# Channels ordered by depth, bands built in two stages, and four PSUM banks in a fused convolution and attention kernel

## The reference

```python
x = _L0_conv_ref(x, L0_conv_W, L0_conv_b)                 # adds a position term
x = x + _L1_conv_ref(_gn(x), ...)
t = _to_tokens(x)
t = t + _L2_attn_ref(_ln_t(t), ...)                       # below
t = t + _L2_ffn_ref(...); t = t + _L3_attn_ref(...); t = t + _L3_ffn_ref(...)

# _L1_conv_ref: 8 heads of 8 channels over 256 tokens
q = xt @ Wq.T + bq;  k, v = halves of xt @ Wkv.T + bkv
q, k = (relu(q) + 1e-06) / scale, (relu(k) + 1e-06) / scale
q, k = each cubed, and scaled back to its own norm
kv_state = einsum('bjc,bjd->bcd', k, v)                   # per head
out = einsum('bic,bcd->bid', q, kv_state) / (q . sum(k) + 1e-06)
out = out + depthwise 5x5 convolution of v + dwc_b        # 8 filters, shared by the heads
return out @ Wproj.T + bproj

# _L2_attn_ref: tanh(H W' + b) gives a score e for each token; then, over the batch,
# C[t] = sum_{s<=t} softmax_{s<=t}(e[s]) * H[s]
```

## Time and profile before

| | us |
|---|---|
| median of 3 runs | 1475.98 (1475.4 to 1478.64) |
| span of the profiled execution | 1099.1 |
| median less span | 376.9 |
| stage one | 0 to 33.4 |
| stage two | 33.4 to 110.8 |
| stage three | 110.8 to 158.9 |
| stage four | 158.9 to 230.4 |
| later stages | 230.4 to 1099.1 |

### The profile page before, as it was taken

One profiled execution on the slowest core, in us unless ns is written; L12 is line 12 of the kernel. 1 busy time (PEld: TensorE's weight loads), 2 busy tenths in 40 slices (PEclk: granted clock), 3 DMA queues, 4 the chain that ended last, 5 costly groups with the idle time before them and its releaser, 6 DMA issues. The chain is left out here.

```text
span 1099.1 us, 12315 instructions
## 1 busy us (share of the span) xinstructions
PE 602.3 (55%) x3397; PEld 478.4 (44%) x3397; DVE 698.3 (64%) x1125; ACT 410.9 (37%) x688; POOL 589.1 (54%) x558
## 2 busy tenths in 40 slices
PE   2789776213310588477279841598155884783000
PEld 2774773213310587477144431244044774772000
DVE  6482474686670598478877589775458893885111
ACT  1454225131300576467224232143135773771000
POOL 0242141420777778777477600677205777775775
PEclk9979887555555799699679865698557996996555
DMA  3000991000211698688261100011104985882211
GB/s 106 7 1 1 207 354 25 0 1 0 94 46 52 198 292 243 198 249 241 57 103 24 24 1 0 38 46 53 53 22 147 299 259 185 261 250 62 55 35 38
DMA packets 126199, 118.91 MB, mean 108 GB/s; under 512 B 24917, under 2 KB 111525, under 8 KB 126147
## 3 DMA queue, kind: packets, MB, share of 16 engines
q1 hardware_dynamic: 56104, 54.93, 16.5%
q10 hardware_dynamic: 53659, 38.16, 11.9%
q0 software_dynamic: 16384, 25.20, 8.4%
HBM read 42.73 MB, written 44.04 MB: 79 GB/s over the span
## 5 line engine op out<-in xcount | busy, mean ns | idle before, releaser
L980 POOL DMA_INDIRECT blocks_x<-L_ffnmhl,L_ffnslot x192 | 198.5, 1034 | 162.9 <-DVE L_ffnslot L1233 105.0
L992 POOL DMA_INDIRECT gy_last<-blocks_y,L_ffnslot x128 | 129.7, 1013 | 57.0 <-issue 38.4
L992 POOL DMA_INDIRECT L_ffngy<-blocks_y,L_ffnslot x128 | 128.1, 1001 | 39.0 <-issue 39.0
L1033 PE MATMUL L_ffnps<-ident,L_ffnxb 128*128 128x128 f32 x384 | 65.5, 300 | 128.3 <-DMA L_ffnxb<-blocks_x 118.6
L1249 DVE TENSOR_TENSOR L_ffnwr<-L_ffnwb,L_ffnwr 128x640 fp32r<-128x640 f32 x96 | 79.2, 826 | 69.7 <-ACT L_ffnwr L1102 68.9
L1049 PE MATMUL L_ffnps<-L_ffnxt,L_ffnwr 128*128 128x256 f32 x768 | 118.3, 299 | 3.0 <-ACT L_ffngate L1118 2.4
L980 POOL DMA_INDIRECT blocks_x<-L_ffnlhl,L_ffnslot x64 | 66.3, 1036 | 82.3 <-DVE L_ffnslot L1233 63.1
L1102 ACT CAST L_ffnwr<-L_ffnwb 128x640 fp32r<-128x640 f32 x96 | 69.8, 727 | 108.5 <-issue 86.5
L1033 PEld LDWEIGHTS L_ffnps<-ident,L_ffnxb 128*128 128x128 f32 x384 | 44.7, 151 | 138.7 <-issue 107.8
L1049 PEld LDWEIGHTS L_ffnps<-L_ffnxt,L_ffnwr 128*128 128x128 f32 x768 | 101.4, 197 | 4.5 <-issue 3.2
L1060 PE MATMUL L_ffnps<-L_ffnwr,L_ffnhlo 128*128 128x128 f32 x384 | 92.8, 280 | 0.0
(11 more groups left out here) (289 smaller groups left out, 1387.4 us busy)
## 6 DMA issues: line engine op xcount, KB each, us to landing
L_ffnwb<-WR SPq DMA_DIRECT2D x192, 160.0 KB, 3.4
L_ffnxb<-blocks_x ACTq DMA_DIRECT2D x96, 256.0 KB
blocks_x<-zeros SPq DMA_DIRECT2D x2, 6144.0 KB, 29.9
blocks_y<-L_ffnyb ACTq DMA_DIRECT2D x96, 128.0 KB
WR<-in_L_ffn_w SPq DMA_DIRECT2D x10, 512.0 KB, 11.0
blocks_x<-L_ffnmhl,L_ffnslot POOLq DMA_INDIRECT x192, 2.2
Xc<-in_x SPq DMA_DIRECT2D x4, 512.0 KB, 7.5
L_ffngy<-blocks_y,L_ffnslot POOLq DMA_INDIRECT x128
```

The costliest lines, as they stand in the source:

```text
L980: pool.indirect_dma_start(self.XD[part], bass.IndirectOffsetOnAxis(self.slot[:, part, k, t:t + 1], 0), self.HL[part][:, t].rearrange("p a ...
L992: pool.indirect_dma_start(self.GY[part][:, k, t], None, self.YD[part], bass.IndirectOffsetOnAxis(self.slot[:, part, k, t:t + 1], 0)).then_ ...
L1033: ins = pe.transpose(ps[:, j % 2, s * P:(s + 1) * P], self.xb[:, j % 4, s], K["ident"][:])
```

## The change

1. Channels inside a head group are ordered by depth and then head: the weights, the bias rows, `epsv`, Wproj and the mask are permuted as they are built. One depth of V is then runs of eight adjacent floats. For Wproj, GpSimd permutes a copy (`w3` to `w2`), and TensorE's transposes wait for it.
2. Bands 0 to 3 are built in stage one: `rowk` is copied earlier, TensorE makes the bands behind the matmul for the means, into banks 4 to 7, and ScalarE copies them ahead of its normalisations. `sely` is loaded in stage one, ahead of four tables on SP's queue. Bands 4 to 7 are built inside the loop over half tiles, ahead of half tiles 16, 20, 24 and 28.
3. The convolution uses the four banks 4 to 7, so TensorE may be four ahead of ScalarE. ScalarE's list is written anew.
4. `mask` and `bp` are loaded in stage two, and SP waits for them there; VectorE's wait in stage three is gone.
5. `add` goes over X in X's order, and BH is the strided operand.

```diff
+BANDS = 4
+
...
+def by_depth(ap):
+    return ap.rearrange("p (h d) -> p d h", d=HD)
+
+
+def heads(ap):
+    return ap.rearrange("p (d h) -> p d h", d=HD)
...
-                pool.memset(K["ones"][:].bitcast(F32), 1.0)
+                then(pool.memset(K["ones"][:].bitcast(F32), 1.0))
+                pool.wait_ge(big_w, 16 * 12)
+                pool.tensor_copy(w2[C:P].rearrange("p a (d h) -> p a d h", d=HD),
+                                 w3[C:P].rearrange("p a (h d) -> p a d h", d=HD)).then_inc(turned, 1)
+                pool.wait_ge(turned, 1)
...
-                    act.dma_start(w2[C:P, half, :], A["L1_conv_Wproj"]).then_inc(big_w, 16)
+                    act.dma_start(w3[C:P, half, :], A["L1_conv_Wproj"]).then_inc(big_w, 16)
...
+                def bands(k):
+                    pj, i4 = k // 4, (k % 4) * 4
+                    act.wait_ge(band_ps, k + 1)
+                    act.copy(T[:, pj, :, i4 * 8:(i4 + 4) * 8].rearrange("p a (u b) -> p u a b", b=8),
+                             ps[:, 4 + k, :].rearrange("p (u a b) -> p u a b", u=4, b=8))
+
+                for k in range(BANDS):
+                    bands(k)
                 act.wait_ge(norm_ready, 1)
                 for q in range(1, Q, 2):
                     act.activation(xn[:, q, :], Xc[:, q, :], ACT.Identity, bias=nmr[:, q:q + 1], scale=rs[:, q:q + 1])
...
                 pe.wait_ge(big_w, 16 * 12)
+                pe.wait_ge(turned, 1)
                 pe.transpose(ps[:, 1, 0:P], w1[:].rearrange("p a c -> p (a c)"), K["ident"][:])
                 pe.transpose(ps[:, 1, P:2 * P], w2[:].rearrange("p a c -> p (a c)"), K["ident"][:]).then_inc(wt_ready, 1)
...
                           start=True, stop=True).then_inc(gm_ready, 1)
+                pe.wait_ge(sely_in, 16)
+                pe.wait_ge(rowk_sb, 1)
+                for k in range(BANDS):
+                    pj, i4 = k // 4, (k % 4) * 4
+                    for u in range(4):
+                        s0 = (HH - 1 - (i4 + u)) * 8
+                        ins = pe.matmul(ps[:, 4 + k, u * P:(u + 1) * P], sely[:, pj, s0:s0 + P],
+                                        rowk[:].rearrange("k d a b -> k (d a b)"), start=True, stop=True)
+                    ins.then_inc(band_ps, 1)

             @block.vector
...
-                dve.tensor_scalar(epsv[:], sp_[:, 7, :], 1e-6, None, ALU.mult)
+                dve.tensor_scalar(heads(epsv[:]), by_depth(sp_[:, 7, :]), 1e-6, None, ALU.mult)
...
+                dve.wait_ge(rowk_ps, 1)
+                dve.tensor_copy(rowk[:], ps[0:KS * WW, 2, 0:P].rearrange("k (b a d) -> k d a b", a=2, d=8)
+                                ).then_inc(rowk_sb, 1)
...
                     rows = slice(b2 * C, b2 * C + C)
                     for k in range(2):
-                        dve.tensor_tensor(wqkv[rows, k, b2, :], ps[rows, 1, k * C:(k + 1) * C], sp_[rows, 7, :], ALU.mult)
-                    dve.tensor_copy(wqkv[rows, 2, b2, :], ps[rows, 1, 2 * C:3 * C])
+                        dve.tensor_tensor(heads(wqkv[rows, k, b2, :]), by_depth(ps[rows, 1, k * C:(k + 1) * C]),
+                                          by_depth(sp_[rows, 7, :]), ALU.mult)
+                    dve.tensor_copy(heads(wqkv[rows, 2, b2, :]), by_depth(ps[rows, 1, 2 * C:3 * C]))
                     dve.tensor_copy(wproj[rows, b2, :], ps[rows, 1, 3 * C:4 * C])
...
-                    then(dve.tensor_copy(brow[row], braw[row]))
-                then(dve.tensor_tensor(brow[row], braw[row], brow[row].bitcast(F32), ALU.subtract))
-                dve.wait_ge(rowk_ps, 1)
-                dve.tensor_copy(rowk[:], ps[0:KS * WW, 2, 0:P].rearrange("k (b a d) -> k d a b", a=2, d=8))
+                    then(dve.tensor_copy(sorted_heads(brow[row]), unsorted_heads(braw[row])))
+                then(dve.tensor_tensor(sorted_heads(brow[row]), unsorted_heads(braw[row]),
+                                       sorted_heads(brow[row]).bitcast(F32), ALU.subtract))
...
+        def of_depth(t, par, d):
+            return t[:, :, par, 0:2 * C].rearrange("p q (b c) -> p q b c", c=C)[:, :, :, d * NH:(d + 1) * NH]
...
-                sp.dma_start(sely[:], A["k_sely"]).then_inc(loaded, 16)
                 sp.dma_start(dwb[:], A["L1_conv_dwc_b"].rearrange("(a d) -> a d", a=1).to_broadcast([P, HD])
                              ).then_inc(loaded, 16)
+                sp.dma_start(mask[:], A["k_mask"]).then_inc(mask_in, 16)
+                for b2 in range(2):
+                    sp.dma_start(bp[:, b2, :], A["L1_conv_bproj"].rearrange("(a c) -> a c", a=1).to_broadcast([P, C])
+                                 ).then_inc(mask_in, 16)
+                sp.wait_ge(mask_in, 48)
...
+                def bands(k):
+                    pj, i4 = k // 4, (k % 4) * 4
+                    if k >= BANDS + 2:
+                        pe.wait_ge(band_sb, k - BANDS - 1)
+                    for u in range(4):
+                        s0 = (HH - 1 - (i4 + u)) * 8
+                        ins = pe.matmul(ps[:, 6 + k % 2, u * P:(u + 1) * P], sely[:, pj, s0:s0 + P],
+                                        rowk[:].rearrange("k d a b -> k (d a b)"), start=True, stop=True)
+                    ins.then_inc(band_ps, 1)
+
                 for i in range(NT2):
+                    if i >= 16 and i % 4 == 0:
+                        bands(BANDS + i // 4 - 4)
...
-                for k in range(8):
-                    pj, i4 = k // 4, (k % 4) * 4
-                    if k >= 2:
-                        pe.wait_ge(band_sb, k - 1)
...
-                    ins.then_inc(band_ps, 1)
                 pe.wait_ge(v_ev, Q // 2)
-                pe.wait_ge(band_sb, 8)
+                pe.wait_ge(band_sb, 8 - BANDS)

                 for k in range(2 * HD):
                     d, pi = k // 2, k % 2
-                    if k >= 2:
-                        pe.wait_ge(conv_ev, k - 1)
+                    if k >= 4:
+                        pe.wait_ge(conv_ev, k - 3)
                     for pj in range(2):
-                        ins = pe.matmul(ps[:, 4 + k % 2, 0:B * NH], T[:, pj, 2 * d + pi, :],
-                                        V[:, :, pj, d:2 * C:HD], start=(pj == 0), stop=(pj == 1))
+                        ins = pe.matmul(ps[:, 4 + k % 4, 0:B * NH], T[:, pj, 2 * d + pi, :],
+                                        of_depth(V, pj, d), start=(pj == 0), stop=(pj == 1))
                     ins.then_inc(conv_mm, 1)

...
                     act.copy(T[:, pj, :, i4 * 8:(i4 + 4) * 8].rearrange("p a (u b) -> p u a b", b=8),
                              ps[:, 6 + k % 2, :].rearrange("p (u a b) -> p u a b", u=4, b=8)).then_inc(band_sb, 1)

                 def conv(k):
                     d, pi = k // 2, k % 2
                     act.wait_ge(conv_mm, k + 1)
-                    act.activation(FM[:, :, pi, d:2 * C:HD], ps[:, 4 + k % 2, 0:B * NH].rearrange("p (q h) -> p q h", q=Q),
+                    act.activation(of_depth(FM, pi, d),
+                                   ps[:, 4 + k % 4, 0:B * NH].rearrange("p (q b h) -> p q b h", q=Q, b=2),
                                    ACT.Identity, bias=dwb[:, d:d + 1]).then_inc(conv_ev, 1)

                 for g in range(G):
...
-
-                        act.wait_ge(loaded, 32)
-                        bands(0)
-                        bands(1)
+                    if g >= 2:
+                        bands(BANDS + 2 * g - 4)
+                        bands(BANDS + 2 * g - 3)
                     act.wait_ge(qk_ev, (g + 1) * QG)
                     square(g)
                     if g == G - 1:
-                        bands(2)
+                        act.wait_ge(loaded, 16)
+                        conv(0)
+                        conv(1)
                     if g >= 1:
                         sixths(g - 1)
                     if g == G - 1:
-                        bands(3)
+                        for k in range(2, 5):
+                            conv(k)
                     if g >= 2:
                         root(g - 2)
-                for k in range(4, 8):
-                    bands(k)
+                for k in range(5, 8):
+                    conv(k)
                 sixths(G - 1)
-                conv(0)
+                conv(8)
                 root(G - 2)
-                for k in range(1, 4):
+                for k in range(9, 12):
                     conv(k)
                 root(G - 1)
-                for k in range(4, 2 * HD):
+                for k in range(12, 2 * HD):
                     conv(k)

             def cube(eng, g):
...
-                dve.wait_ge(loaded, 48)
                 for q in range(Q):
                     dve.wait_ge(kv_mm, q + 1)
-                    dve.tensor_tensor(BD[:, q, 0:P], ps[:, 4 + q % 2, 0:P], mask[:], ALU.mult)
-                    dve.tensor_tensor(BD[:, q, P:W], mask[:, 0:P:HD], ps[:, 4 + q % 2, P:P + 1].to_broadcast([P, 2 * NH]),
+                    m = mask[:].rearrange("p (b c) -> p b c", b=2)
```

(21 more changed lines are left out.)

49 lines of the change are left out of this document (22 added, 27 removed).

## The result

The changed kernel took 1458.42 us (1453.33 to 1460.19, 4 runs) beside 1477.31 for the kernel before (1475.4 to 1480.24, 4 runs): ratio 0.9865, 95% interval 0.983 to 0.99. The forecast was 1458.1, and it started from 1475.98, the median of three of these four runs before; against 1477.31 the saving is 18.9 us. The span of the profiled execution is 1458.4 us.

What follows compares the result with a forecast made beforehand. Bounds were read stage by stage from what ends last, with TensorE's convolution bounding stage two; 3.8 - 16.1 - 5.4 - 0.2 = -17.9 from 1475.98 gave 1458.1 us, range 1451 to 1466.

Steps and rivals of the forecast that it cites:

- Stage one: First stage: bands 0 to 3 at TensorE's low clock delay ScalarE's normalisations, +3.8 us (bounds +0.8 to +5.3).
- Stage two: Second stage: faster convolution records leave VectorE and GpSimd setting the end, 94.4 against 110.5, -16.1 us.
- the delay by the copies in ScalarE's queue: Second stage: band copies ahead of ScalarE's squares make the sixths begin at 73.65 in place of 71.17, +2.5 us.
- a check at 0.356: Second stage's convolution: it would be late again only above 0.356 us a record; 0.245 was assumed.
- rival (a): Second stage's convolution: reading rate isn't the stride's, records stay at 0.46 us; total 1463.6 us, chance 0.09.
- Rival (b): Second stage: clock falls while TensorE waits for bands 6 and 7, VectorE slips 2.5 to 4; 1461.5 us, chance 0.11.
- Stage three: Third stage: VectorE no longer waits for mask and bias loads; 12.2 to 13.9 us where 18.5 was taken, -5.4 us.
- the start at the low clock: Third stage: TensorE starts low; a pair of tiles costs 2.74 us, 1.33 at full clock; one to two rises allowed.
- Stage four: Fourth stage's sums: VectorE and GpSimd exclude each other, so contiguous X brings hardly anything, -0.2 us.
- the sign to look for: Fourth stage: sums still one after the other, near 9.3 us from the last scan to the stage's end.
- Rival (c): Fourth stage: sums get what their new order seems to promise, -3.6 us; total 1454.7 us, chance 0.13.
- 376.9 us lie outside the span: Whole kernel before: span 1099.1 us against median 1475.98; the difference was kept, and savings in the span subtracted from the median.

Runs made afterwards that it cites:

- e10: Changed kernel with unread matmuls keeping TensorE busy in stage one, its pauses filled too; 1075.91 us beside 1097.91 for the kernel before, ratio 0.9807.
- e1: Changed kernel with its channels again ordered head by head, as in the kernel before; ratio 0.9888 to the kernel before.
- e7: Changed kernel with the convolution in two PSUM banks in place of four; one execution, no timed ratio, stage two 61.4 us.
- e11: Changed kernel again, unaltered, on a chip with the short later stages; 1081.89 us beside 1099.08 for the kernel before, ratio 0.9832.
- e5: Changed kernel again, unaltered, beside the kernel before on the same chip; 1460.8 us beside 1475.13, ratio 0.9874.
- e9: Kernel before again, unaltered, for its trace; 1098.71 us, with a span of 1097.1 us.
- e4: Changed kernel with both products and both sums of stage four on VectorE, none on GpSimd; ratio 0.9781 to the kernel before.

## Why the prediction held, point by point

**Stage one** (+3.8): +4.0, 37.4 for 33.4. Copies 1.71 apart, normalisations behind them, low clock: as read from the earlier trace rows; e10 confirms the clock as the cause, and its normalisations end at 33.94, where the prediction had 33.9 for the high level.

**Stage two** (-16.1, length 61): 61.8, so -15.6. All was some 0.6 us later than worked out, because the low clock at the stage's start lasted 5.6 us (37.46 to 43.05) where I had counted the 3.5 of before. The order of events is the forecast's: the delay by the copies in ScalarE's queue (2.5 us forecast; counted from the stage's start, the sixths come 2.9 later than before), VectorE and GpSimd setting the end, and VectorE's L462 waiting for GpSimd's scaling. The record was 0.22, for which I had 0.245 and a check at 0.356. e1 shows what rival (a) would have cost: 6.8 us, for which I had 6.6. Rival (b) had its hole (1.74 us ahead of 75.70), and the clock stayed at 1.00 in it and behind it. The hole of 4.02 us before 90.32 I hadn't seen: the granted clock is still 1.00 in it and 0.69 from 90.32 to 95.8, with no harm, as the convolution had slack. The Trainium skill's rule on 16-byte lines (SBUF — State Buffer, "Door 1: The DMA port swizzle") agrees: runs of eight take 0.22 us a record, no more than the contiguous 0.245, and a stride of 32 bytes 0.46.

The four banks were named in the sum as what lets TensorE be ahead of ScalarE. That was so and was worth about 0.5 us (e7): slack beyond what the path needs gains nothing. I should have priced two banks as well.

**Stage three** (-5.4): -7.8 here, for a length of 40.3. The term mis-sized is the start at the low clock, which I took as certain. In the trace after it didn't occur. In e11, the same kernel, it did, TensorE in stage three:

```profile
99.38 2.06 PE L501 MATMUL a_ps<-V,QKf 128*128 128x129 f32 x8 [3.54 <-PEq L301]
...
102.09 1.93 PE L501 MATMUL a_ps<-V,QKf 128*128 128x129 f32 x8
...
104.67 1.17 PE L501 MATMUL a_ps<-V,QKf 128*128 128x129 f32 x8
```

With two pairs at the low clock the stage took 43.0 there (42.7 forecast). In e5 (41.9) the first pair was at the high clock and the second at the low. All three occur: 40.3, 41.9 and 43 in the table. A term like that should be a set of values with chances, not one.

**Stage four** (-0.2): -1.6, 70.0 us for 71.6. The sums are 0.7 of it: from the last scan to the end 9.06 us for 9.75, where the term (-0.2) and the sign to look for (9.3) did not even agree with each other. The other 0.9 lies ahead of the sums, where nothing was changed, and did not come again (70.8 and 70.9 in e5 and e11, 71.2 in e9). Rival (c), 3.6 us from the order alone, is out: in order of X or not, the sums wait for each other, and e4 shows the price of that, 3.4 us. The Trainium skill's lock (SBUF — State Buffer, "Who interferes with whom") is borne out on both sides: by 8.76 us for a sum beside GpSimd's, 3.6 (7.17 / 2) without.

**The sum.** -17.9 was forecast. The traces give -20.9 for the first pair, and -18.0 for e9 and e11 (231.2 - 213.2); the timed ratios give 0.9865 and 0.9832, 19.9 and 18.5 us. So the near hit of 0.3 us is partly luck: stages three and four won 2.4 and 1.4 more than forecast in this trace, the timed median less than the trace, and the base was a median of three runs 1.3 us below that of four. Runs of one kernel on one chip spread by far more than 0.3 us (1453.33 to 1460.19 here, 1441.32 to 1466.72 in e5).

**What was wrong** is the statement that 376.9 us lie outside the span. The span after is 1458.4 beside a time of 1460.19: 1.8 us lie outside. The profile of before (1099.1) and its timed runs (1475.98) must then come from executions of the two lengths told of below: the kernel before takes 1475.13 beside e5 and 1098.71, with a span of 1097.1, in e9. That is an inference, as no run has both. It did no harm to the sum only because the change lies ahead of the stages in which the two lengths differ; had it touched GpSimd's gathers, prices read from that profile would not have held for the timed runs.

## What to carry to other kernels

Read each stage by what ends last, and price an edit by the chain that takes over when that is gone: here 15.6 us came off TensorE's end before VectorE and GpSimd became the bound, and more banks for TensorE behind that point brought about 0.5. Where VectorE and GpSimd both read two tensors from SBUF at the same time, try all of it on VectorE: 3.4 us less in e4. In stage one TensorE ran at its low clock, and matmuls moved there cost double until its pauses were filled with unread ones (e10): look at the duration of a known matmul in the stage that work is moved to, and compare a profile's span with the timed runs of its own chip before anything is said of what lies outside it.
